# Query stage of a two-layer kernel: weight sums moved to VectorE, another scale for the weights, tokens kept by phase within 128, output steps that work in PSUM

## The reference, cut to what matters

```python
qkv = x @ w_qkv.T                                  # q: 1024 channels, k: 256, v: 256
q = causal_conv1d(causal_conv1d(q, qc1_w, qc1_b, 16), qc2_w, qc2_b, 1)
k = causal_conv1d(causal_conv1d(k, kc1_w, kc1_b, 4), kc2_w, kc2_b, 1)
q = q.reshape(B, S, 16, 64) + 0.5 * k_mean[:, :, None, :]
k = k.reshape(B, S, 4, 64) + 0.5 * q_mean[:, :, None, :]
q, k = l2norm(q), l2norm(k) * key_temp
q, k = rope(q, cos, sin), rope(k, cos, sin)
scores = einsum('bhqd,bhkd->bhqk', q, kg) * 64 ** -0.5   # causal mask, softmax
out = einsum('bhqk,bhkd->bhqd', attn, vg) ... @ w_o.T
```

## Time and profile before

| | us |
|---|---|
| median of 3 runs | 2455.86 (2452.49 to 2457.8) |
| the profiled execution | 2458.84 |
| its span, first to last instruction | 2457.0 |
| query stage in it | about 611 to 1148 |
| attend, middle | about 1148 to 1461, 1461 to 1748 |

### The profile page before, as it was taken

One profiled execution on the slowest core, in us unless ns is written; L12 is line 12 of the kernel. 1 busy time (PEld: TensorE's weight loads), 2 busy tenths in 40 slices (PEclk: granted clock), 3 DMA queues, 4 the chain that ended last, 5 costly groups with the idle time before them and its releaser, 6 DMA issues. The chain is left out here.

```text
span 2457.0 us, 46530 instructions
## 1 busy us (share of the span) xinstructions
PE 2083.3 (85%) x19144; PEld 1014.4 (41%) x19144; DVE 1493.2 (61%) x2928; ACT 1113.1 (45%) x1939; POOL 891.0 (36%) x775
## 2 busy tenths in 40 slices
PE   7999989998537778884999979997588888888879
PEld 3444445555213333332555534444244444444434
DVE  3543354333368777664778752455788888888813
ACT  1221145454223323313767730223267777777760
POOL 0210301222656776743444420223434334334410
PEclk9999999999778888886999989998699999999999
DMA  6020101101312211015222144222663544644424
GB/s 231 35 86 35 64 27 39 39 15 56 114 50 60 67 45 43 18 26 190 67 77 87 66 163 169 77 63 84 130 143 61 78 76 63 83 75 62 68 68 147
DMA packets 136184, 193.26 MB, mean 79 GB/s; under 512 B 43490, under 2 KB 74852, under 8 KB 133412
## 3 DMA queue, kind: packets, MB, share of 16 engines
q1 hardware_dynamic: 134388, 176.65, 27.9%
...
HBM read 129.94 MB, written 60.29 MB: 77 GB/s over the span
## 5 line engine op out<-in xcount | busy, mean ns | idle before, releaser
L3011 DVE TENSOR_REDUCE f_chunk_max<-f_ps_a 128x64 f32<-128x1024 f32 x320 | 319.5, 1032 | 49.9 <-PE f_ps_a L2755 27.0
L2884 ACT ACTIVATE conv_in<-f_ps_s 128x512 f32<-128x512 f32 x480 | 258.4, 602 | 89.4 <-PE f_ps_s L2786 45.4
L2755 PE MATMUL f_ps_a<-conv_in 128*32 128x512 bf16 (+3 forms) x3072 | 201.7, 342 | 40.1 <-DVE f_chunk_max L3011 25.3
L1981 ACT ACTIVATE d_probs<-d_ps_s,d_shift 128x512 f32<-128x512 f32 (+3 forms) x384 | 196.6, 584 | 82.7 <-PE d_ps_s L1920 72.5
L2786 PE MATMUL f_ps_s<-f_qs,f_ks 128*32 128x512 bf16 x2304 | 209.0, 385 | 25.9 <-ACT f_qs L2875 14.6
L1369 PE MATMUL c_ps_c<-conv_in,c_wT 128*128 128x512 f16 x768 | 195.7, 411 | 12.7 <-DVE c_wT L1609 12.7
L2951 POOL TENSOR_SCALAR f_absent<-f_rest 128x576 f32<-128x576 f32 x32 | 54.4, 1699 | 302.4 <-DVE f_rest L3028 178.2
L2808 PE MATMUL f_ps_o<-conv_in,f_v 128*32 128x512 f32 (+2 forms) x1152 | 125.3, 522 | 27.4 <-ACT conv_in L2884 27.4
L2875 ACT ACTIVATE f_qs<-f_ps_s 32x512 bf16<-32x512 f32 x192 | 112.8, 587 | 75.4 <-PE f_ps_s L2769 71.2
L1931 PE MATMUL d_ps_o<-d_probs,conv_in 128*64 128x512 f32 (+3 forms) x768 | 146.1, 488 | 0.0
L2755 PEld LDWEIGHTS f_ps_a<-conv_in 128*32 128x32 bf16 x3072 | 72.6, 98 | 162.2 <-DVE f_chunk_max L3011 66.6
...
## 6 DMA issues: line engine op xcount, KB each, us to landing
...
```

The costliest lines, as they stand in the source:

```text
L1981: act.activation(probs[n % RING][SCORES[c][1]][:, lo:hi], ps_s[c % BANKS][:, lo - hi + CH:], ACT.Exp, bias=shift[:, 0:1], scale=HD0 ** -0. ...
L2755: last = pe.matmul(out[side(e), h, 0:w], qa[u][:, 2 * p + h, side(e, qt * P)], ka[u][:, kh * CH:kh * CH + w], start=True, stop=not last_keys)
L2884: act.activation(probs[m % HELD][:, :, at:at + P], bank_of["s", i, n][:].rearrange("p (h n) -> p h n", n=P), ACT.Exp, scale=HD1 ** -0.5).t ...
L3011: dve.tensor_reduce(chunk_max[:, qt - 2, :, at:at + w // CHUNK], src.rearrange("p h (c k) -> p h c k", k=CHUNK), AX.X, ALU.max).then_inc(a ...
```

## The change: what it does

1. **Weight sums.** The six sums of a tile are formed on VectorE by `sums(k, i)` (two TENSOR_TENSOR, four SCALAR_TENSOR_TENSOR, all 128x1024 f32). GpSimd's six and ScalarE's `twice` and `fourfold` are gone.
2. **Scale.** ScalarE squares the three taps of a tile with a running sum (`ends_of`, three ACTIVATE of 128x1024), three narrow matmuls with a matrix of ones add over partitions and taps (`bound`), VectorE copies the number (`size_of`), GpSimd takes its power -1/2 (`root`, 128x1), and `scales` follows. `extremes`, `tallest`, `find_peak` and `share_peak` are gone.
3. **Tokens.** They are kept by phase within each 128 tokens (four runs of 32, `RUN = 32`) from the project stage's stores to the middle stage. `parts` and `remainder` read and write plain columns. The project stage stores `k_raw` and `k_mean` in runs of 64 tokens. Attend loads each batch of `v` with four transfers of 32 partitions, and uses a mask turned to match. Middle loads `g` and `x` with four transfers of 32 partitions each per chunk, stores `x1` so, and its transposes have an identity with turned columns, which puts tokens back in order.
4. **Output steps.** `combine(m, 3)` writes into the PSUM banks of slices 2 and 3, and four steps of `combine(m, 2)` read these banks and two write them. The buffer `even[1]` is gone. Those two banks come free later, after step 11 and step 10 of 13 of the tile. The ring `ps_c` has four banks and the spread of norms (`ps_b`) two instead of three.
5. `turned` has two buffers, so `rotate(g)` waits for the rest of unit g-2 and not of g-1. The order on all engines is written anew; the hooks of a tile are at h = (1, 2, 3, 7, 8, 10) instead of (1, 2, 3, 4, 5, 8), and `bound(m + 2)` at h = 11 takes the place of `find_peak` at 8 and `share_peak` at 10.

The core of the diff:

```diff
-        even = [sb(f"even{i}", [P, CH]) for i in range(2)]
-        odd = [sb(f"odd{i}", [P, CH]) for i in range(2)]
+        even = sb("even", [P, CH])
+        spent = square[0][:].bitcast(BF16)
+        odd = [sb("odd", [P, CH]), square[1]]
-        turned = sb("turned", [P, S])
+        turned = [sb(f"turned{i}", [P, S]) for i in range(2)]
-        RING, SPREADS = 3, 3
+        RING, SPREADS = 4, 2
...
+            def bound(k):
+                pe.wait_ge(ends_summed, TAPS * (k + 1))
...
+                for a in range(TAPS):
+                    last = pe.matmul(ps_x[:, 0:1], ones[:], ends[k % 2][:, a:a + 1], start=(a == 0), stop=(a == TAPS - 1))
+                last.then_inc(bound_done, 1)
-            HOOKS = (1, 2, 3, 4, 5, 8)
-            PEAK_AT, SHARE_AT = 8, 10
+            HOOKS = (1, 2, 3, 7, 8, 10)
+            BOUND_AT = 11
...
-                if i in (0, 2):
-                    return copied, 2 * m + 1 + (i == 2)
-                return y_step, Y_STEPS * m + {1: 2, 3: 4, 4: 12, 5: 13}[i]
+                if i == 0:
+                    return copied, 2 * m + 1
+                return y_step, Y_STEPS * m + {1: 2, 2: 11, 3: 10, 4: 12, 5: 13}[i]
...
-                act.activation(in_time(part_of(g, 0)), by_phase(turned_of(g)), ACT.Copy).then_inc(high_ready, 1)
+                act.activation(part_of(g, 0), turned_of(g), ACT.Copy).then_inc(high_ready, 1)
...
+            def sums(k, i):
+                a0, a1, a2 = [rows[k % 2][:, a] for a in range(TAPS)]
+                s0, s1 = sums_of[0][:], sums_of[1][:]
+                to, first, by, second = ((s0, a2, 1.0, a0), (s1, a1, 1.0, s0), (s0, a1, -1.0, s0),
+                                         (s1, a2, 4.0, a0), (s0, a1, 2.0, s1), (s1, a1, -2.0, s1))[i]
...
+                if by == 1.0:
+                    dve.tensor_tensor(to, first, second, ALU.add).then_inc(w_sum, 1)
+                else:
+                    dve.scalar_tensor_tensor(to, first, by, second, ALU.mult, ALU.add).then_inc(w_sum, 1)
...
-                    dve.scalar_tensor_tensor(out[:, :, 1, :], runs(odd[1][:]), 2.0, runs(odd[0][:]), ALU.mult, ALU.add).then_inc(y_step, 1)
+                    dve.scalar_tensor_tensor(of_phase(raw, 1), runs(src), 2.0, runs(odd[0][:]), ALU.mult, ALU.add).then_inc(y_step, 1)
...
-        sp.dma_start(self.g_in[c % 2], tokens("g")).then_inc(self.loaded[c % 2], 16)
-        sp.dma_start(self.x_in[c % 2], tokens("x")).then_inc(self.loaded[c % 2], 16)
+        for to, name in ((self.g_in, "g"), (self.x_in, "x")):
+            for j in range(PHASES):
+                sp.dma_start(to[c % 2][j * RUN:(j + 1) * RUN], turned_rows(self.dram[name], c, j)).then_inc(self.loaded[c % 2], 16)
```

385 lines of the change are left out of this document (193 added, 192 removed).

## The result

| | before | after |
|---|---|---|
| median of the runs, us | 2455.69 | 2369.54 (2361.19 to 2372.51, 4 runs) |
| profiled execution, span, us | 2457.0 | 2370.7 |
| ratio to before, 95% interval | | 0.9645, 0.9617 to 0.9673 |
| granted clock over the span | 0.931 | 0.944 |

A forecast was written before the change was run, and what follows sets the result against it. VectorE, late through waits behind GpSimd on shared SBUF ports, was taken as the bound. Terms -31 - 11 - 25 - 2.6 + 0.5 + 3 = -66 took 2458.84 to 2393, adjusted to 2390 for the runs' median; range 2350 to 2428.

The forecast's parts named there:

- What bounded before: Query stage: TensorE stops 8.12 us for the peak because VectorE is late, its two-SBUF-input steps waiting for running GpSimd instructions.
- the shared pair: SBUF ports of VectorE and GpSimd: locked for a whole instruction, needed by VectorE when two inputs lie in SBUF.
- Tiles 1 to 6: Steady tiles of the query stage: from 323.5 us to 6 x 48.7 = 292, a change of -31.
- if the power holds the pair it waits 4.3: Steady tile: a VectorE `lows` beside GpSimd's power of norms waits 4.3 us; bounds 0 and 5.5 a tile.
- The walk: Steady tile: the new order stepped through once, both engines taking the ports in turn; 48.7 us, or 43.5 without the power's wait.
- Rival A: Steady tile: the power does not hold the ports, 43.5 us a tile, kernel 2359; chance 0.20 for 2345 to 2372.
- Tile 7: Last tile of the query stage: set by TensorE, 49.3 us becomes 38, a change of -11.
- Tile 0: First tile, from the tables' landing at 626.05: ends at 715 instead of 740.51, -25, trusted least, +-10.
- `remainder`, `parts`, steps that write PSUM: Query stage: `remainder` 1.2 us and `parts` 1.1 alone; a 512-column step writing PSUM 0.65, like reading it.
- Transfers of 32 partitions: First loads of `g` and `x` ahead of middle: half rate, 5 us more, of which 3 show; bounds 0 and +13.
- Middle: Middle stage after its first matmul: no change, 0.
- Tail: End of the query stage: last `parts` and `remainder`, 2.50 and 2.43 us, become 1.1 and 1.2, -2.6.

The follow-up runs named there:

- b_tallest_early: The kernel before, with VectorE's `tallest(m+2)` ahead of `combine(m, 2)` instead of behind it: 2459.97 us, ratio 1.0025 to before.
- a_sums_pool: The kernel after, with the six weight sums on GpSimd again, without three sums' factors: 2402.81 us, ratio 0.9788 to before.
- p_ports: The kernel after plus a first stage timing VectorE steps beside GpSimd instructions: 16 two-input steps, eight of them beside powers, take 20.19 us, 1.26 each.
- f_stores: f_best (after, reordered tiles, two middle edits; 2331.11 us), with SyncE storing each unit's high part before its low part, separate semaphores: 2326.46 us, ratio 0.9478 to before.
- a_one_transfer: The kernel after, with middle's `g` and `x` loaded in one 128-partition transfer each instead of four of 32: 2362.64 us, ratio 0.9628 to before.
- a_plain_ident: The kernel after, with middle's transposes against a contiguous identity instead of one read with a stride: 2360.92 us, ratio 0.9620 to before.

## Why the prediction was right, and where it was not

- **What bounded before: right in the main.** TensorE's stop was slack (b_tallest_early), and VectorE's waits behind GpSimd are in the rows. But the prediction explained VectorE's lateness by the shared pair alone. VectorE also waited for what ScalarE, TensorE and GpSimd make late, and in a_sums_pool one late sum costs 8.0 us a tile where the pair costs 0.8 more than in after.
- **Tiles 1 to 6, -31 forecast, -67.6 measured.** The mechanism was right, one term of the sum was not: "if the power holds the pair it waits 4.3". It waits 0 (p_ports, and 1.28 beside the power). I had one row, a power 0.93 us longer behind a VectorE step, from which follows that the power needs the pair, and I let the wide instructions decide how long it keeps it. The walk without it gave 43.5, measured 42.6. Rival A's 2359 had the place and nearly the size; I gave it 0.20 and took the other value.
- **That 43.5 came so near is partly luck.** In the tiles of 42.5 us VectorE waits 6.1 us behind GpSimd where the sum had 14.1: 4.3 less for the power, 2.9 less for the second rotation (0.9 instead of 3.8) and 0.9 less for the first. It waits 2.2 instead of 2.9 for ScalarE. Against that stand 2.0 us for the spread of the norms (`c_ps_b`), which the sum put beside VectorE and at nothing, and 0.5 more of its own work.
- **The walk's order: right.** The rotation behind `raw`, the norms step at 15.2 after it (15.8 forecast), the first sums' waits.
- **Tile 7: right**, 38.1 against 38.
- **Tile 0, -25 forecast, -18.8 measured.** Counted from the scale step, `units(0)` starts at 28.4 (forecast 30), norms 1 at 63.2 (65), `combine(0, 2)` at 71.9 (73.4). Only behind that the walk misses 7 us: ScalarE's next `parts` waits for the stores of the keys' low part, and VectorE's `remainder` for it. The walk had engines and no stores. f_stores takes 3.1 of them back.
- **`remainder`, `parts`, steps that write PSUM: right**, 1.23, 1.06 and 0.76.
- **Transfers of 32 partitions: right in kind.** They move at half rate (208 to 211 GB/s), 5.4 us show, of which 5.0 are theirs (a_one_transfer); I had said that 3 of the 5 show, but the last store stands behind all of them.
- **Middle, 0 forecast, +5.6 measured: missed.** I read the turned identity as an edit without cost. Read with a stride, it makes each transpose 397 ns instead of 273 (a_plain_ident).
- **Tail, -2.6 forecast, -1.0 measured**; I made no run on it.
- **The sum.** The error of tiles 1 to 6 (-37) and those of the rest (+16, of which tile 0 +6, middle +6, attend's end +2, tail +2) partly cancel; 2390 was 20 us too high. That it was not 37 too high is luck.
